# A 64-row contraction piece padded with zeros to 128 rows in the routed experts' return product

## The chip, the core and the metric

The kernel runs on one core of one Trainium2 chip. The metric is the device time of one execution in microseconds (us); lower is better. The kernel is one program for the whole model, and the change touches two of its six stages.

## What is computed

The input is 16 sequences of 256 tokens with 128 features. Six layers follow one another: a routed feed-forward, a retention layer, the routed feed-forward again, a relative-attention layer with its own experts, a plain attention and the relative layer again. The change lies in the routed feed-forward. Cut to what matters, it is:

```python
capacity = int(T / E * CAPACITY_FACTOR)            # 256 tokens / 8 experts * 1.25 = 40
scales = softmax(h @ rW3 + rb3)                    # router, three dense layers
topk_scales, topk_experts = top_k(scales, 2)
pos = ...                                          # place of each token in its expert's queue
keep = pos < capacity
dispatched = zeros((E, B, capacity, C)).at[e_flat, b_idx, pos_c].set(where(keep, x_rep, 0))
hh = relu(einsum('ebnc,ech->ebnh', dispatched, eW1) + eb1)
eout = einsum('ebnh,ehc->ebnc', hh, eW2) + eb2
out = sum(topk_scales[..., None] * where(keep, eout[e_flat, b_idx, pos_c], 0), axis=2)
x = x + 0.5 * out
```

The last two lines bring the experts' outputs back to the tokens. For one sequence there are 8 experts x 40 places = 320 slots, and each token's result is a weighted sum over those 320 slots (at most two weights are not zero).

## The kernel before

`routed_ffn` (line 107 on) is called twice, as stage f1 (from the start of the program) and as stage f3 (after the retention stage). It works on 8 groups of 2 sequences; a group is 4 tiles of 128 tokens (`GT = 4`). Its outer loop runs over steps s = 0 to 10, written out by hand for each engine. In step s the router works on group s, group s - 1 gets its slots, and the experts work on a pair of groups q two steps later. Each engine carries out its own list in the order written, and semaphores tie the lists together.

The return product is `back(q, half)` on TensorE (PE in the profile). It multiplies the slot weights of a group (`gts`, slots x tokens) with the experts' outputs (`eos`, slots x features). The contraction runs over 320 slots, and TensorE contracts at most 128 rows at once, so it is cut in three pieces:

```python
CHUNKS = [(first, min(P, S - first)) for first in range(0, S, P)]   # (0,128) (128,128) (256,64)
NW, WHOLE, LEFT = len(CHUNKS), S // P, S % P                        # 3, 2, 64
```

For each of the 4 token tiles `back` issues three matmuls of 128, 128 and 64 rows, which add up in one PSUM region. The operands are fp32, and the trace shows each such matmul as two, so that one `back` is 24 matmuls in the trace, all at line 358. The two `back` of a pair q stand in the even steps 4, 6, 8 and 10. In steps 4 and 6 the order on PE is: turning of the experts' outputs (`turn_slots`, line 345), a router product (`layer2`, lines 254 to 258), `back` of the first half, `count` (lines 290, 291), a router product (lines 214 to 216), `back` of the second half, `slots` (line 300), then `hidden` (line 312). In step 8 the router has ended and its products fall out; in step 10 only `turn_slots` and the two `back` are left.

What `back` gives is taken by VectorE (DVE) in `residual` (line 708), which adds half of it to `x`. In steps 4, 6 and 8 VectorE then does `place` (lines 657 and 662), which makes the table `f_d` that `slots` on TensorE needs; `count` needs `f_mask` (line 649). In step 10 a memset (line 763) stands between the two `residual`, and GpSimd (POOL) has one more (line 851).

The operands of `back` are written by copies from PSUM: lines 505, 506 (ScalarE, ACT) and 702, 703 (VectorE) for `eos`, lines 497, 498 and 696, 697 for the three buffers of `gts`. Lines 506, 703, 498 and 697 write only rows 0 to 63 of the third piece. One buffer of `gts` is `f_gts`; the other two lie in a tile that another stage owns, and appear as `all_qs`.

GpSimd's list starts with `ln_root(0)` (lines 800, 802: the reciprocal root for the layer norm), `rest_of_x(0)` (line 813) and four `rest_of_h1(0, m)` (line 819); then its loop over steps begins with `ln_root(1)`. VectorE's `ln_apply(1)` (line 597) waits for `ln_root(1)`, and TensorE's `turn_x(1)` (line 209) waits for `ln_apply(1)`.

Of the kernel before, what the change touches and what calls it, by code (L numbers as in the profile page):

```python
# [27 lines left out]
P = 128  # L28
B, T, C = 16, 256, 128
TT = T // P  # L30
# [3 lines left out]
KH = HID // P  # L34
# [72 lines left out]
def routed_ffn(nc, tag, x_sb, k, w):  # L107
# [3 lines left out]
    CHUNKS = [(first, min(P, S - first)) for first in range(0, S, P)]  # L111
    NW, WHOLE, LEFT = len(CHUNKS), S // P, S % P
    XW = NB * CAP
    W = GT * P
    HR, KR = 4, 3
    x_g = x_sb[:, :, :].rearrange("p (g t) c -> p g t c", t=GT)
    with ExitStack() as ctx:
        a = Pool_(nc, ctx, tag)
# [18 lines left out]
        eos, own = a.sb("eos", [P, NB, NW, C]), a.sb("gts", [P, GT, NW, P])  # L137
        stack = [k.qs[:, n, :, :].rearrange("p h t -> p (h t)").bitcast(F32) for n in range(2)]
        turned = [half[:, 0:GT * NW * P].rearrange("p (t v c) -> p t v c", t=GT, v=NW) for half in stack]
        gts = [turned[0], own, turned[1]]  # L140

        orders = {"ra": [], "rv": [], "ea": [], "ev": []}
        for s in range(G + 3):
            group, q, e = s - 1, (s - 2) // 2, 4 * (s % 2)
# [35 lines left out]
        def ring(name):  # L180
            taken = a.sem(f"{name}_taken")
            names = {item for item, _ in orders[name]}
            return Bench(a.ps(name, [P, 2, 512]), a.sem(f"{name}_filled"), {item: taken for item in names}, orders[name])

        ra, rv, ea, ev = ring("ra"), ring("rv"), ring("ea"), ring("ev")
        ra_taken, rv_taken, ea_taken, ev_taken = ra.emptied["x"], rv.emptied["h1"], ea.emptied["slots"], ev.emptied["slots"]
        (ln_stats, ln_aggr, ln_veps, ln_rstd, xn_ready, top_ready, lg_ready, ex_ready, den_step, sc_ready, best_step,
         mask_step, off_ready, d_ready, g_ready, xt_ready, h1_ready, zeroed, ks_zeroed) = [a.sem(n) for n in (
             "ln_stats ln_aggr ln_veps ln_rstd xn_ready top_ready lg_ready ex_ready den_step sc_ready best_step "
             "mask_step off_ready d_ready g_ready xt_ready h1_ready zeroed ks_zeroed").split()]  # L190
        block = ctx.enter_context(nc.Block())
        ROUTE = (ra, rv, ra, rv)
        EXPERT = (ea, ev)
# [1 line left out]
        @block.sync  # L195
        def _(sp):
            if w.load is not None:
                w.load_router(sp)
                w.load_rest(sp)
                w.load(sp)  # L200
                w.load_positions(sp)

        @block.tensor
        def _(pe):
# [144 lines left out]
            def back(q, half):  # L349
                g = 2 * q + half  # L350
                ev.free(pe, "back", (q, half))
                for b in range(2):
                    EXPERT[b].done(pe, "eos", (q, 2 * half + b))
                ea.done(pe, "weights", (g, 2))
                ev.done(pe, "weights", (g, 3))
                for t in range(GT):
                    for v, (first, rows) in enumerate(CHUNKS):
                        mm = nc.tensor.matmul(ev.bank("back", (q, half))[:, t * P:(t + 1) * P], gts[g % KR][0:rows, t, v, :],
                                              eos[0:rows, 2 * half + t // TT, v, :], start=(v == 0), stop=(v == NW - 1))
                mm.then_inc(ev.filled, 1)  # L360

            pe.wait_ge(k.loaded, k.loaded_count)
            for s in range(G + 3):
                group, q, e = s - 1, (s - 2) // 2, 4 * (s % 2)
# [35 lines left out]
                else:  # L400
# [4 lines left out]
                    if closed:  # L405
                        back(q - 1, 0)
# [4 lines left out]
                    if closed:  # L411
                        back(q - 1, 1)
# [383 lines left out]
        @block.gpsimd  # L796
        def _(pool):
            def ln_root(g):
                pool.wait_ge(ln_aggr, g + 1)
                nc.gpsimd.tensor_tensor(veps[:, :], mv[:, :, 1], k.eps[:, 0:GT], ALU.add).then_inc(ln_veps, 1)  # L800
                pool.wait_ge(ln_veps, g + 1)
                nc.gpsimd.tensor_tensor(rstd[:, :], veps[:, :], k.minus_half[:, 0:GT], ALU.pow).then_inc(ln_rstd, 1)

            def weigh(g):
                EXPERT[1].full(pool, "slots", (g, 1))
                nc.gpsimd.tensor_tensor(d[:, :, :], d[:, :, :], sc[:, :, :].rearrange("p t e -> p (t e)").unsqueeze(2)
                                        .to_broadcast([P, GT * E0, CAP]), ALU.mult).then_inc(g_ready, 1)

            def rest_of_x(g):
                ra.done(pool, "x", g)  # L810
                if g:
                    ROUTE[3].full(pool, "h1", (g - 1, 3))
                nc.gpsimd.tensor_tensor(xt_lo[:, :], xt[:, :], xt_hi[:, :], ALU.subtract).then_inc(xt_ready, 1)

            def rest_of_h1(g, m):
                ROUTE[m].done(pool, "h1", (g, m))
                if g:
                    ROUTE[3].full(pool, "h2", (g - 1, 3))
                nc.gpsimd.tensor_tensor(h1_lo[:, m, :], h1[:, m, :], h1_hi[:, m, :], ALU.subtract).then_inc(h1_ready, 1)

            pool.wait_ge(k.loaded, k.loaded_count)
            ln_root(0)
            rest_of_x(0)
            for m in range(KH):
                rest_of_h1(0, m)
            for s in range(G + 1):
                if s < G - 1:
                    ln_root(s + 1)
                if s and s % 2 == 0:
                    weigh(s - 1)  # L830
                if s < G - 1:
                    rest_of_x(s + 1)
                if s % 2:
                    weigh(s - 1)
                if s < G - 1:
                    for m in range(KH):
                        rest_of_h1(s + 1, m)
                if s == 1 and w.load is not None:
                    pool.wait_ge(h1_ready, 3 * KH)
                    for n, rows in enumerate((slice(32, 64), slice(64, ROWS))):  # L840
                        nc.gpsimd.memset(w.ws[rows, :, :, :].rearrange("p a h t -> p (a h t)"), 0.0).then_inc(w.ws_zeroed, 1)
                        pool.wait_ge(w.ws_zeroed, n + 1)
            pool.wait_ge(g_ready, G)
            if w.load is not None:
                for n, rows in enumerate((slice(32, 64), slice(64, ROWS))):
                    nc.gpsimd.memset(k.ks[rows, :, :, :].rearrange("p a h t -> p (a h t)"), 0.0).then_inc(ks_zeroed, 1)
                    pool.wait_ge(ks_zeroed, n + 1)
            for n, (last, tile, rows) in enumerate((((G // 2 - 2, 1), stack[1], slice(32, 64)), ((G // 2 - 2, 1), stack[1], slice(64, ROWS)),
                                                    ((G // 2 - 1, 0), stack[0], slice(64, ROWS)))):
                EXPERT[1].full(pool, "back", last)  # L850
                nc.gpsimd.memset(tile[rows, :], 0.0).then_inc(zeroed, 1)
                pool.wait_ge(zeroed, n + 1)
# [2403 lines left out]
def program(nc, io, stages=(1, 2, 3, 4, 5, 6)):  # L3256
    with ExitStack() as ctx:
        a = Pool_(nc, ctx, "all")
        x_sb = a.sb("x", [P, B * TT, C])
        k = constants(nc, a, io["cst"])  # L3260
        w = Weights()
        positions_weights(nc, a, io, w)
        with ExitStack() as layer:
            layer0_weights(nc, Pool_(nc, layer, "l0"), io, w)
            load_x(nc, k, io["x"], x_sb, w)
            if 1 in stages:
                routed_ffn(nc, "f1", x_sb, k, w)
                w.load = None
            if 2 in stages:
                retention(nc, "r2", x_sb, k, io)  # L3270
            if 3 in stages:
                routed_ffn(nc, "f3", x_sb, k, w)
        with ExitStack() as early:
            b = Pool_(nc, early, "a5b")
            x2t = b.sb("x2t", [P, B * TT, P])
            begun = Forerun(nc, b, "a5b", x_sb, k, io, x2t)
            relative_ffn(nc, "f4", x_sb, k, w, io, x2t=x2t, then=begun)
            relative_ffn(nc, "f6", x_sb, k, w, io, lambda lead, room: plain_attention(nc, "a5", x_sb, k, io, begun, lead, room), x2t=x2t,
                         out=io["out"])
# [75 lines left out]
```

## Time and profile before

| | |
|---|---|
| three timed runs | 3012.8, 3013.13, 3018.33 us; median 3013.13 us |
| the profiled execution: its own time, its span | 3010.51 us, 3008.5 us |
| mean granted TensorE clock | 0.974 |
| busy share of the span: PE, weight loads, DVE, ACT, POOL | 94%, 75%, 65%, 62%, 68% |

The span is the time from the first to the last instruction of one profiled execution; it is the time against which rows are set. Stage f1 takes the first 308 us of it, stage f3 the stretch from 523 to 820 us. A matmul's row shows its start and a modelled end: matmuls overlap, one of 128 columns is shown with some 275 ns, and the next starts long before that has passed. So the pace is read from start to start, not from the duration. "PEld" rows are the weight loads that belong to the matmuls; "idle before" in brackets names what an engine waited for.

### The profile page before, as it was taken

How to read it: one execution, taken by the hardware profiler on the slowest of the kernel's cores; microseconds unless marked ns; L12 is line 12 of the kernel's file. 1: busy time of each engine (PE TensorE's matmuls, PEld its weight loads, DVE VectorE, ACT ScalarE, POOL GpSimd, SP SyncE). 2: the span in 40 equal slices, each digit the busy share in tenths (PEclk: the TensorE clock that was granted, in tenths of full speed). 3: DMA queues.
4: the chain of work that ended last, by engine and by line, in shares of the span. 5: the costliest groups of instructions: out<-in, count | busy, mean ns of one | idle time of the engine just before them, and what ended most of it. 6: DMA issues, size and time to landing. Idle time of an engine off the chain costs nothing. (4 is left out here: it accounts for less than half of the span.)

```text
span 3008.5 us, 61670 instructions
## 1 busy us (share of the span) xinstructions
PE 2831.6 (94%) x20928; PEld 2262.6 (75%) x20928; DVE 1950.5 (65%) x4370; ACT 1851.2 (62%) x5109; POOL 2033.7 (68%) x2542
## 2 busy tenths in 40 slices
PE   7999797899879999998999989998999999999999
PEld 5888565688768888886788856665888888778887
DVE  5554587445458888886555566774888888755554
ACT  2333343333269999996444446777999999754444
POOL 4323664323168888876999974555888888689998
PEclk9999899999989999999999989999999999999999
DMA  3000464000032222222554555552222222255554
GB/s 109 6 1 1 115 142 98 1 1 1 10 64 44 43 44 54 54 58 104 182 193 185 188 166 118 113 104 47 43 50 58 43 44 43 57 205 194 195 194 165
DMA packets 152505, 266.05 MB, mean 88 GB/s; under 512 B 14098, under 2 KB 124946, under 8 KB 129138
## 3 DMA queue, kind: packets, MB, share of 16 engines
q1 hardware_dynamic: 152194, 262.11, 31.1%
q8 instruction: 170, 2.79, 0.4%
q14 instruction: 141, 1.16, 0.1%
HBM read 204.06 MB, written 53.67 MB: 86 GB/s over the span
## 5 line engine op out<-in xcount | busy, mean ns | idle before, releaser
L3144 POOL TENSOR_TENSOR f4m_ht_lo<-f4m_ht,f4m_ht_hi 128x512 fp32r<-128x512 f32 x256 | 331.0, 1311 | 38.2 <-ACT f4m_ht_hi L3069 29.0
L3144 POOL TENSOR_TENSOR f6m_ht_lo<-f6m_ht,f6m_ht_hi 128x512 fp32r<-128x512 f32 x256 | 331.2, 1307 | 32.3 <-ACT f6m_ht_hi L3069 20.2
L3114 DVE SCALAR_TENSOR_TENSOR f6m_ht<-f6m_hr,f6m_gate 128x512 f32<-128x512 f32 x256 | 176.3, 690 | 168.0 <-PE f6m_hr L2991 104.5
L3114 DVE SCALAR_TENSOR_TENSOR f4m_ht<-f4m_hr,f4m_gate 128x512 f32<-128x512 f32 x256 | 175.6, 690 | 162.3 <-PE f4m_hr L2991 101.9
L3069 ACT ACTIVATE f4m_ht_hi<-f4m_ht 128x512 fp32r<-128x512 f32 x256 | 161.6, 632 | 193.1 <-DVE f4m_ht L3114 192.8
L3069 ACT ACTIVATE f6m_ht_hi<-f6m_ht 128x512 fp32r<-128x512 f32 x256 | 161.7, 632 | 191.2 <-DVE f6m_ht L3114 191.0
L2665 ACT ACTIVATE f4a_pr<-f4a_sr,f4a_nm 128x256 f32<-128x256 f32 x512 | 243.7, 497 | 23.3 <-DVE f4a_nm L2733 22.8
L2665 ACT ACTIVATE f6a_pr<-f6a_sr,f6a_nm 128x256 f32<-128x256 f32 x512 | 243.6, 496 | 21.2 <-DVE f6a_nm L2733 20.5
L2819 POOL TENSOR_TENSOR f4a_rr<-f4a_tmp 128x256 f32<-128x256 f32 x256 | 186.7, 729 | 92.5 <-DVE f4a_tmp L2741 91.3
L2819 POOL TENSOR_TENSOR f6a_rr<-f6a_tmp 128x256 f32<-128x256 f32 x256 | 186.8, 730 | 82.8 <-DVE f6a_tmp L2741 81.6
L2741 DVE TENSOR_TENSOR f4a_tmp<-f4a_ur,f4a_turn 128x512 f32<-128x512 f32 x256 | 175.1, 685 | 61.2 <-PE f4a_ur L2530 57.4
L1997 DVE TENSOR_REDUCE a_nm<-a_sr 128x2 f32<-128x512 f32 x256 | 166.9, 684 | 69.3 <-PE a_sr L1730 68.2
L2733 DVE TENSOR_REDUCE f6a_nm<-f6a_sr 128x2 f32<-128x512 f32 x256 | 175.8, 687 | 50.5 <-PE f6a_sr L2547 49.6
L2733 DVE TENSOR_REDUCE f4a_nm<-f4a_sr 128x2 f32<-128x512 f32 x256 | 175.8, 687 | 50.1 <-PE f4a_sr L2547 49.3
L2741 DVE TENSOR_TENSOR f6a_tmp<-f6a_ur,f6l_turn 128x512 f32<-128x512 f32 x256 | 175.1, 684 | 49.2 <-PE f6a_ur L2530 46.6
L2825 POOL TENSOR_TENSOR f6a_rr_lo<-f6a_rr,f6a_rr_hi 128x256 fp32r<-128x256 f32 x256 | 190.4, 744 | 1.3 <-ACT f6a_rr_hi L2706 1.3
L2825 POOL TENSOR_TENSOR f4a_rr_lo<-f4a_rr,f4a_rr_hi 128x256 fp32r<-128x256 f32 x256 | 190.4, 744 | 0.9 <-ACT f4a_rr_hi L2706 0.9
L2545 PE MATMUL f4a_sr<-f4a_pe_hi,f4a_rr_hi 128*128 128x256 f32 x512 | 187.6, 366 | 0.0
L2545 PE MATMUL f6a_sr<-f6l_pe_hi,f6a_rr_hi 128*128 128x256 f32 x512 | 187.5, 366 | 0.0
L2557 PE MATMUL f6a_tr<-all_table,f6a_pr 128*128 128x128 f32 x1024 | 153.6, 272 | 0.3 <-ACT f6a_pr L2665 0.3
L2557 PE MATMUL f4a_tr<-all_table,f4a_pr 128*128 128x128 f32 x1024 | 153.5, 272 | 0.3 <-ACT f4a_pr L2665 0.3
L2542 PE MATMUL f4a_sr<-all_ks,all_qs 96*128 96x256 bf16 x512 | 143.4, 280 | 5.8 <-POOL f4a_rr_lo L2825 3.6
(585 smaller groups left out, 9368.5 us busy)
## 6 DMA issues: line engine op xcount, KB each, us to landing
f4m_gate<-f4o_gates SPq DMA_DIRECT2D x64, 1024.0 KB, 4.7
f6m_gate<-f6o_gates SPq DMA_DIRECT2D x64, 1024.0 KB, 4.7
r_scratch<-r_parts SPq DMA_DIRECT2D x32, 192.0 KB, 2.2
all_qs<-r_scratch SPq DMA_DIRECT2D x16, 384.0 KB, 4.9
all_ks<-r_scratch SPq DMA_DIRECT2D x16, 384.0 KB, 6.8
f4al_scratch<-f4a_parts SPq DMA_DIRECT2D x32, 192.0 KB, 2.2
all_qs<-f4al_scratch SPq DMA_DIRECT2D x16, 384.0 KB, 4.9
all_ks<-f4al_scratch SPq DMA_DIRECT2D x16, 384.0 KB, 6.7
```

Source lines behind the costliest of these rows:

```text
L1997: nc.vector.tensor_reduce(nm[:, r // 2, t, at_:at_ + 2], sr[:, g % SB, :].rearrange("p (x s) -> p x s", x=2), AX.X, ALU.max, negate=True). ...
L2542: nc.tensor.matmul(out, qs[0:ROWS, lead.buffer(b[0]), h, t * P:(t + 1) * P], ks[0:ROWS, lead.buffer(b[0]), h, :], start=True, stop=False)
L2545: nc.tensor.matmul(out, rr_hi[at], pe_hi[:, :], start=False, stop=False)
L2557: mm = nc.tensor.transpose(ring.bank(b, n // 2)[:, o:o + P], pr[:, n % 4, x, st * P:(st + 1) * P], k.ident)
L2665: last = nc.scalar.activation(pr[:, n % 4, x, :], sr.bank(b, n)[:, x * T:(x + 1) * T], ACT.Exp, bias=nm[:, n % SB, x:x + 1], accum_out=zs[ ...
L2733: nc.vector.tensor_reduce(nm[:, n % SB, :], sr.bank(b, n).rearrange("p (x s) -> p x s", x=2), AX.X, ALU.max, negate=True).then_inc(nm_read ...
L2741: nc.vector.tensor_tensor(tmp[:, hs % 2, :, :], ur.bank(b, hs).rearrange("p (u t) -> p u t", u=2), turn[:, :, :], ALU.mult).then_inc(ur.em ...
L2819: nc.gpsimd.tensor_tensor(rr[:, hs % RAW, :], tmp[:, hs % 2, 0, :], tmp[:, hs % 2, 1, :], ALU.add)\
L2825: nc.gpsimd.tensor_tensor(rr_lo[:, hs % RRS, :], rr[:, hs % RAW, :], rr_hi[:, hs % RRS, :], ALU.subtract)\
L3069: nc.scalar.activation(ht_hi[:, n % RB, :], ht[:, n % RB, :], ACT.Copy).then_inc(hi_ready, 1)
L3114: nc.vector.scalar_tensor_tensor(ht[:, n % RB, :], hr[:, n % HB, :], 0.0, gate[:, q % GB, n % LOADED, :], ALU.max, ALU.mult).then_inc(ht_r ...
L3144: nc.gpsimd.tensor_tensor(ht_lo[:, n % RB, :], ht[:, n % RB, :], ht_hi[:, n % RB, :], ALU.subtract)\
```

## The change

The third piece is contracted over 128 rows as the others are. Rows 64 to 127 of its operands are filled with zeros, so that the product is the same. GpSimd writes these zeros once per stage, into `eos` and the three buffers of `gts`: four memsets of 64 partitions x 4 x 128 fp32. They stand behind the four `rest_of_h1(0, m)` and ahead of `ln_root(1)`, and each waits for the one before it. TensorE waits for all four (`padded` at 4) before the first `back` of the stage. The copies that write rows 0 to 63 stay as they are, and nothing writes rows 64 to 127 later in the stage.

```diff
@@ back, on TensorE
+                if q == 0 and half == 0:
+                    pe.wait_ge(padded, 1 + KR)
                 for t in range(GT):
-                    for v, (first, rows) in enumerate(CHUNKS):
-                        mm = nc.tensor.matmul(ev.bank("back", (q, half))[:, t * P:(t + 1) * P], gts[g % KR][0:rows, t, v, :],
-                                              eos[0:rows, 2 * half + t // TT, v, :], start=(v == 0), stop=(v == NW - 1))
+                    for v in range(NW):
+                        mm = nc.tensor.matmul(ev.bank("back", (q, half))[:, t * P:(t + 1) * P], gts[g % KR][:, t, v, :],
+                                              eos[:, 2 * half + t // TT, v, :], start=(v == 0), stop=(v == NW - 1))
@@ GpSimd's list
             for m in range(KH):
                 rest_of_h1(0, m)
+            pool.wait_ge(h1_ready, KH)
+            for n, tile in enumerate([eos] + gts):
+                nc.gpsimd.memset(tile[LEFT:P, :, WHOLE, :], 0.0).then_inc(padded, 1)
+                pool.wait_ge(padded, n + 1)
             for s in range(G + 1):
                 if s < G - 1:
                     ln_root(s + 1)
```

`padded` is also added to the list of the stage's semaphores. GpSimd's list at the start of stage f1, before (`f_h_lo` is written by `rest_of_h1`, `f_veps` and `f_rstd` by `ln_root(1)`):

```order
L819 TENSOR_TENSOR f_h_lo<-f_h,f_h_hi 128x512 [waits load_table_in]
L819 TENSOR_TENSOR f_h_lo<-f_h,f_h_hi 128x512 [waits f1_rv_taken]
L800 TENSOR_TENSOR f_veps<-f_mv,all_half 128x4 [waits f1_ln_aggr]
L802 TENSOR_TENSOR f_rstd<-f_veps,all_half 128x4 [waits f1_ln_veps]
L813 TENSOR_TENSOR f_xt_lo<-f_xt,f_xt_hi 128x512 [waits f1_rv_filled,load_table_in]
```

and in the changed kernel (lines are some lines further down there):

```order
L821 TENSOR_TENSOR f_h_lo<-f_h,f_h_hi 128x512 [waits load_table_in]
L821 TENSOR_TENSOR f_h_lo<-f_h,f_h_hi 128x512 [waits f1_rv_taken]
L830 MEMSET f_eos 64x4x128 [waits f1_h1_ready]
L830 MEMSET all_qs 64x4x128 [waits f1_padded]
L830 MEMSET f_gts 64x4x128 [waits f1_padded]
L830 MEMSET all_qs 64x4x128 [waits f1_padded]
L802 TENSOR_TENSOR f_veps<-f_mv,all_half 128x4 [waits f1_ln_aggr,f1_padded]
L804 TENSOR_TENSOR f_rstd<-f_veps,all_half 128x4 [waits f1_ln_veps]
L815 TENSOR_TENSOR f_xt_lo<-f_xt,f_xt_hi 128x512 [waits f1_rv_filled,load_table_in]
```

Four instructions come in, and what followed stands four places later. On TensorE nothing moves. The piece of its list around the first `back` of the stage, with the old rows and the new ones:

```order
 L255 MATMUL f_ra<-f_h_hi,l_rw_lo 128x512
 L258 MATMUL f_ra<-f_h_lo,l_rw_hi 128x512 [waits f1_h1_ready] x4
-L358 MATMUL f_ev<-f_eos,all_qs 128x128 [waits f1_ea_taken,f1_ev_taken]
-L358 MATMUL f_ev<-f_eos,all_qs 128x128 x11
+L360 MATMUL f_ev<-f_eos,all_qs 128x128 [waits f1_ea_taken,f1_ev_taken,f1_padded]
+L360 MATMUL f_ev<-f_eos,all_qs 128x128 x11
 L291 MATMUL f_rv<-f_mask,all_bf 128x8 [waits f1_mask_step,f1_rv_taken]
 L290 MATMUL f_rv<-f_mask,all_bf 128x8
```

The twelve matmuls of a `back` keep their place and number; the first of the stage has one more semaphore to wait for, and every third one now has 128 rows.

## Rows read from the trace of the kernel before

**Rows 1.** Busy time by stretch, f1 and f3: length, busy us (count) per engine, PE clock.
```profile
118.00:308.00 190.00, 185.31 (x1126) 154.30 (x1125) 91.11 (x305) 55.61 (x148) 61.85 (x37) 1.00 0.00 1
628.00:823.00 195.00, 187.40 (x1137) 155.96 (x1135) 91.83 (x310) 56.05 (x148) 48.81 (x39) 1.00 0.01 2
```

**Rows 2.** Waits of PE from 118 to 310 us: us in total, times, longest.
```profile
PE f_ea L312 <- issue: 1.9, 3, 0.6
PE f_ea L345 <- issue: 0.8, 1, 0.8
```

**Rows 3.** Line 358 in f1 by shape: count, busy us, mean ns, idle before.
```profile
L358 PE MATMUL f_ev<-f_eos,all_qs 128*128 128x128 f32 x80 | 13.9, 296 | 0.2 <-DVE f_eos L703 0.2
L358 PE MATMUL f_ev<-f_eos,all_qs 64*128 64x128 f32 x40 | 9.7, 323 | 0.0
```

**Rows 4.** Timeline, weight loads of the first `back`, step 4: start, length in us, count.
```profile
133.90 0.29 PEld L358 LDWEIGHTS f_ev<-f_eos,all_qs 64*128 64x128 f32 x2
134.32 0.52 PEld L358 LDWEIGHTS f_ev<-f_eos,all_qs 128*128 128x128 f32 x4
134.96 0.29 PEld L358 LDWEIGHTS f_ev<-f_eos,all_qs 64*128 64x128 f32 x2
```

**Rows 5.** Timeline, TensorE around the two `back` of step 4.
```profile
133.37 4.19 PE L358 MATMUL f_ev<-f_eos,all_qs 128*128 128x128 f32 x24
...
137.49 0.18 PE L291 MATMUL f_rv<-f_mask,all_bf 128*128 128x8 bf16 x1
...
140.53 4.19 PE L358 MATMUL f_ev<-f_eos,f_gts 128*128 128x128 f32 x24
```

**Rows 6.** Timeline, step 4: `residual`, `place`, then `slots` on TensorE.
```profile
137.60 0.69 DVE L708 SCALAR_TENSOR_TENSOR all_x<-f_ev,all_x 128x512 f32<-128x512 f32 x1 [2.99 <-PE f_ev L358]
...
138.42 1.49 DVE L662 TENSOR_TENSOR f_d<-all_table,f_pos 128x1280 f32<-128x1280 f32 x1
...
144.65 1.34 PE L300 MATMUL f_ea<-f_d,f_xn 128*128 128x320 f32 x4
```

**Rows 7.** Timeline, step 8: `back`, mask, `residual`, `place`, `slots`.
```profile
265.25 4.27 PE L358 MATMUL f_ev<-f_eos,f_gts 128*128 128x128 f32 x24 [0.21 <-ACT f_eos L506]
...
267.56 0.18 DVE L649 TENSOR_SCALAR f_mask<-f_left 128x32 bf16<-128x32 f32 x1
...
269.56 0.69 DVE L708 SCALAR_TENSOR_TENSOR all_x<-f_ev,all_x 128x512 f32<-128x512 f32 x1 [1.60 <-PE f_ev L358]
...
270.38 1.49 DVE L662 TENSOR_TENSOR f_d<-all_table,f_pos 128x1280 f32<-128x1280 f32 x1
...
273.83 1.34 PE L300 MATMUL f_ea<-f_d,f_xn 128*128 128x320 f32 x4
```

**Rows 8.** Timeline, step 10, end of f1, and the next stage's first memset.
```profile
298.35 4.27 PE L358 MATMUL f_ev<-f_eos,all_qs 128*128 128x128 f32 x24 [0.21 <-DVE f_eos L703]
...
302.65 0.69 DVE L708 SCALAR_TENSOR_TENSOR all_x<-f_ev,all_x 128x512 f32<-128x512 f32 x1 [3.86 <-PE f_ev L358]
302.73 1.80 POOL L851 MEMSET all_qs<- 32x2048 f32 x1 [6.41 <-PE f_ev L358]
303.82 1.76 DVE L763 MEMSET all_qs<- 32x2048 f32 x1 [0.48 <-issue]
306.88 0.69 DVE L708 SCALAR_TENSOR_TENSOR all_x<-f_ev,all_x 128x512 f32<-128x512 f32 x1 [1.29 <-PE f_ev L358]
308.43 3.52 POOL L1329 MEMSET r_vm<- 128x4096 f32 x1 [3.90 <-POOLq L75]
```

**Rows 9.** Timeline, start of f1: `ln_root(1)`, `ln_apply(1)`, `turn_x(1)`.
```profile
20.09 0.20 POOL L800 TENSOR_TENSOR f_veps<-f_mv,all_half 128x4 f32<-128x4 f32 x1
...
20.38 1.02 POOL L802 TENSOR_TENSOR f_rstd<-f_veps,all_half 128x4 f32<-128x4 f32 x1
...
24.20 1.11 DVE L597 TENSOR_SCALAR f_xn<-all_x,f_mv,f_rstd 128x128 f32<-128x128 f32 x4
...
28.93 0.60 PE L209 MATMUL f_ra<-all_table,f_xn 128*128 128x128 f32 x4
```

More of the change, by code:

```diff
@@ L187, in routed_ffn @@
         (ln_stats, ln_aggr, ln_veps, ln_rstd, xn_ready, top_ready, lg_ready, ex_ready, den_step, sc_ready, best_step,
-         mask_step, off_ready, d_ready, g_ready, xt_ready, h1_ready, zeroed, ks_zeroed) = [a.sem(n) for n in (
+         mask_step, off_ready, d_ready, g_ready, padded, xt_ready, h1_ready, zeroed, ks_zeroed) = [a.sem(n) for n in (
              "ln_stats ln_aggr ln_veps ln_rstd xn_ready top_ready lg_ready ex_ready den_step sc_ready best_step "
-             "mask_step off_ready d_ready g_ready xt_ready h1_ready zeroed ks_zeroed").split()]
+             "mask_step off_ready d_ready g_ready padded xt_ready h1_ready zeroed ks_zeroed").split()]
         block = ctx.enter_context(nc.Block())
```

## The prediction

> **What bounds the kernel now.** I read the stretches first, then the waits of TensorE inside them, then the matmuls of line 358 by shape, then the single rows around them. In both routed stages the stretch with all the `back` (steps 4 to 10) keeps TensorE busy for 185 of 190 us and 187 of 195 us, at a granted clock of 1.00, while VectorE, ScalarE and GpSimd are busy for under half of it [rows 1]. TensorE's waits there come to 2.7 us in two places, of 0.6 and 0.8 us each [rows 2], and two of 0.21 us before a `back` [rows 7, 8]. So TensorE's own list sets the time of these stretches, and a microsecond taken out of that list is a microsecond of the kernel, as long as nothing that does not itself wait for the shortened part is late.
>
> A busy share says nothing of whether the time is well spent. The shapes of line 358 show a mean of 296 ns with 128 rows and 323 ns with 64 [rows 3], which looks like a small matter. But a duration here is a modelled end; the pace is in the starts. The four weight loads of two 128-row matmuls start at 134.32 and take 0.52 us together [rows 4]; one load is 0.19 us (0.29 us for a pair that starts 0.11 apart reads the same), so (0.52 - 0.19) / 3 = 0.11 us from start to start. That is the pace with no change of shape. After the four comes a pair with 64 rows at 134.96, that is 0.64 us after 134.32 where four times 0.11 would give 0.44. And a pair with 64 rows takes from 133.90 to 134.32, 0.42 us, where two times 0.11 would give 0.22 [rows 4]. Each change of the row count, in either direction, thus costs 0.2 us, and a token tile has two of them: 134.96 - 133.90 = 1.06 us for six matmuls instead of 0.67.
>
> **The change part by part.** *The `back` itself.* One `back` lasts from its first start to the start of what follows: 137.49 - 133.37 = 4.12 us [rows 5]. All 24 matmuls now have 128 rows: 24 x 0.112 = 2.69 us (0.112 and not 0.11, the upper side of what 0.33 / 3 can be by its rounding). It saves 1.43 us. The second one of step 4, 140.53 to 144.65, is 4.12 us too [rows 5, 6]. There are two in each of steps 4, 6, 8 and 10, eight per stage, 16 in all. The pace of a long run of 24 such matmuls isn't shown before, only runs of four; the bounds are 0.107, the lower side of the rounding, and 4.12 / 24 = 0.172, the mean pace of today's mix, which would save 1.55 us and nothing. I take 0.112, since the row nearest to the new list is the one of four equal shapes.
>
> Does the wall follow? *Steps 4 and 6.* `count` waits for the mask, which is there long before. `slots` waits for `place`: in step 4 VectorE waits 2.99 us for the first `back`, then has `f_d` ready at 138.42 + 1.49 = 139.91, and `slots` starts at 144.65 [rows 6]. With both `back` shortened, `slots` could start at 141.79; even an `f_d` that did not move would be there by then. Both savings are kept: 2.86 us per step.
>
> *Step 8.* Here no router product lies between. The first `back` starts at 265.25; `count` then comes at about 265.25 + 2.77 = 268.02 (0.08 more, since this `back` starts after a wait), and the mask is written until 267.56 + 0.18 = 267.74, 0.28 us before. The residual starts at about 268.2 instead of 269.56, and `f_d` ends 2.31 us after that start (270.38 + 1.49 - 269.56), at 270.5. The second `back` ends its starts at about 268.19 + 2.77 = 270.96, so `slots` finds `f_d` 0.4 us old [rows 7]. Both savings are kept, with little room.
>
> *Step 10.* The two `back` run one after the other, so VectorE's first residual moves from 302.65 to about 301.2 and the memset behind it from 303.82 to 302.4, ending at 304.15. The second `back` would let the second residual start 2.86 us early, at 304.0; the memset now ends last. So it starts at 304.15 instead of 306.88: 2.7 us are kept. GpSimd's memset (302.73, 1.80 us) moves along and stays hidden [rows 8].
>
> The stage after starts from a barrier behind these and moves as a whole. Per stage 3 x 2.86 + 2.7 = 11.3 us, for two 22.6 us.
>
> *The memsets.* GpSimd's rows show 1.80 us for 2048 fp32 per partition and 3.52 us for 4096 [rows 8], 0.88 ns per element, with 32 or 128 partitions alike. 512 elements make 0.45 us, four make 1.8, with about 0.1 us between two dependent instructions (20.09 + 0.20 to 20.38 [rows 9]) 2.2 us. They push `ln_root(1)`, which ends at 20.38 + 1.02 = 21.40, to 23.6. `ln_apply(1)` starts at 24.20, because VectorE is at other work: hidden. If the memsets cost more, `turn_x(1)` comes only at 28.93 and `ln_apply` takes 1.11, so `ln_root(1)` may end as late as 27.7 [rows 9]: 6.3 us of cover. The bounds: nothing, and four times the nearest longer row, 7.2 us, which would be 0.9 us late, 1.8 us for two stages. I take nothing. No other engine waits for GpSimd in between, and TensorE's new wait is for something done 100 us before. Stage f3 has the same order at its start.
>
> **Rule and row.** The 64-row matmuls stand off from the 128-row ones by 0.2 us each way [rows 4]. The Trainium skill, "TensorE: Matmul & The Clock Gate", section "LDWEIGHTS (loading the stationary operand)", says the opposite of a gain: a weight load's time goes by its columns, and one of 32 rows takes as long as one of 128; the table in "Why this matters for your kernels" says the same of a single matmul. By that rule padding changes nothing, and the sum would be 0. The rows bear the rule out for the load by itself (0.29 us for a pair) but not for the pace across a change of shape, which is what this kernel pays for.
>
> **The sum.** The profiled execution took 3010.5 us by its own time; less 22.6 that is 2987.9. The median of the timed runs is 3013.1, 2.6 above it, so I predict 2990.5 us.
>
> **The rivals.** *No difference.* A matmul costs by its columns, and the gaps of 0.2 us belong to something else that comes every six matmuls (the new token tile's operands and output). Against it: the gap stands before the 64-row pair as well, inside a tile, where operands and output region go on as before. If only the shown durations differed, 64 x 0.027 us x 2 stages = 3.5 us [rows 3] for the fp32 pairs: 3009.6, which no measurement tells from no change (the bound is 0.2%, 6 us). Chance 0.05.
>
> *A new wait takes part of it.* VectorE's chain mask, residual, `place` becomes the last in step 8 and its memset in step 10, where the room is 0.3 to 0.4 us and none. If the second saving in both steps were lost, 4 x 1.43 less the 0.3 already counted = 5.4 us: 2995.9. For it: the small margins of rows 7 and 8; against it: each link of the chain itself waits for the first `back`, which is earlier too. Chance 0.10.
>
> *Slower.* The memsets on GpSimd hold up `ln_root(1)`, with it `ln_apply(1)` and `turn_x(1)`. Place: the start of f1 and of f3. If one cost the 3.52 us of the longest memset on this engine [rows 8], four would end at 34.3, `ln_root(1)` at 35.5, 7.8 us after the last harmless moment: 15.6 us in both stages. It decides from 1.6 us per memset on, and makes the kernel slower where the gain on TensorE is smaller than the delay, at worst 3013.1 + 15.6 = 3028.7. Against it: an eighth of the elements. Chance 0.03.
>
> The forecast itself has a chance of 0.82.
>
> **How the numbers follow.** A pace of 0.107 us would save 16 x 0.12 = 1.9 us more (2988.6), the memsets at their upper bound 1.8 us less (2992.3), and runs of the kernel before lie up to 5 us apart. The new wait reaches to 2996. I give 2985 to 2998. Faster by over 0.2% are the forecast and the new wait: 0.92; within 0.2% 0.05; slower 0.03.
>
> **What would show it.** In the changed kernel's profile all rows of the return product have 128 rows, and one `back` of 24 reads about 2.8 us instead of 4.19; the first residual of step 4 waits about 1.6 us instead of 2.99; `slots` of step 4 comes 2.9 us sooner after the step's start; the stretch of steps 4 to 10 is 11 us shorter in each of the stages; four memsets of 64 partitions take about 0.5 us each, and `ln_apply(1)` stands where it stood. I am wrong if the rows keep gaps of 0.2 us between token tiles, if `slots` in step 8 waits for `f_d`, or if `turn_x(1)` starts later than before.

## The result

The changed kernel takes 2987.39 us (median of 4 runs, 2985.78 to 2989.39), the kernel before 3013.23 us (4 runs, 3012.8 to 3018.33). The ratio is 0.9911, with a 95% interval of 0.9894 to 0.9928: 25.8 us faster, where 2990.5 us were predicted and 2985 to 2998 was the range. The profiled execution took 2985.78 us with a span of 2983.8 us, 24.7 us less than the span before, at the same mean granted clock of 0.974.

### The profile page after: what moved, and what is told of

Its sections match the earlier page's. It is cut to its first block and busy times, and to the rows that moved or that the text cites. A ratio compares the mean times of both kernels' runs of the same rounds, so it can differ in the third digit from the quotient of the medians.

```text
span 2983.8 us, 61682 instructions
## 1 busy us (share of the span) xinstructions
PE 2806.0 (94%) x20928; PEld 2255.4 (76%) x20928; DVE 1951.9 (65%) x4370; ACT 1852.1 (62%) x5109; POOL 2039.4 (68%) x2550
```

## The profile after

The stretch that answers to [rows 1] for f1, steps 4 to 10, taken 11 us shorter since the stage ends that much earlier (columns as there):

```profile
118.00:297.00 179.00, 173.28 (x1125) 149.79 (x1123) 91.43 (x307) 55.47 (x148) 62.27 (x38) 1.00 0.00 1
```

TensorE is about as full as before (173.3 of 179 us, before 185.3 of 190): 12 us less busy time for nearly the same number of matmuls in the window (1125, before 1126). The length of a window is chosen; what is measured is the time from the first `back` of f1 to its last residual, 306.88 - 133.37 = 173.51 us before and 295.10 - 133.22 = 161.88 us now. The return product by shape and one stretch of its weight loads, answering to [rows 3] and [rows 4]:

```profile
L360 PE MATMUL f_ev<-f_eos,all_qs 128*128 128x128 f32 x120 | 14.4, 276 | 0.2 <-DVE f_eos L705 0.2
L360 PE MATMUL f_ev<-f_eos,f_gts 128*128 128x128 f32 x72 | 8.6, 276 | 0.2 <-ACT f_eos L508 0.2
```
```profile
133.44 0.41 PEld L360 LDWEIGHTS f_ev<-f_eos,all_qs 128*128 128x128 f32 x3
```

All 192 matmuls of the stage have 128 rows and a mean of 276 ns, and three weight loads at a boundary between the second and the third piece take 0.41 us: (0.41 - 0.19) / 2 = 0.11 us from start to start. Before, the load of the third piece stood 0.2 us behind that pace. The timeline around the two `back` of step 4 answers to [rows 5] and [rows 6]:

```profile
133.22 2.84 PE L360 MATMUL f_ev<-f_eos,all_qs 128*128 128x128 f32 x24
...
135.89 0.17 PE L291 MATMUL f_rv<-f_mask,all_bf 128*128 128x8 bf16 x1
...
136.09 0.69 DVE L710 SCALAR_TENSOR_TENSOR all_x<-f_ev,all_x 128x512 f32<-128x512 f32 x1 [1.63 <-PE f_ev L360]
...
136.91 1.49 DVE L664 TENSOR_TENSOR f_d<-all_table,f_pos 128x1280 f32<-128x1280 f32 x1
...
138.92 2.84 PE L360 MATMUL f_ev<-f_eos,f_gts 128*128 128x128 f32 x24
...
141.59 1.24 PE L300 MATMUL f_ea<-f_d,f_xn 128*128 128x320 f32 x4
```

One `back` lasts 135.89 - 133.22 = 2.67 us up to what follows, instead of 4.12. VectorE's residual waits 1.63 us for it instead of 2.99. The second one lasts 2.67 us too (138.92 to 141.59). And `slots` itself reads 1.24 us where it read 1.34: before, it was the first matmul after a 64-row one and paid for the change as well.

Step 8, answering to [rows 7]:

```profile
259.11 2.92 PE L360 MATMUL f_ev<-f_eos,f_gts 128*128 128x128 f32 x24 [0.21 <-ACT f_eos L508]
...
261.42 0.18 DVE L651 TENSOR_SCALAR f_mask<-f_left 128x32 bf16<-128x32 f32 x1
...
261.86 0.17 PE L291 MATMUL f_rv<-f_mask,all_bf 128*128 128x8 bf16 x1
...
262.06 0.69 DVE L710 SCALAR_TENSOR_TENSOR all_x<-f_ev,all_x 128x512 f32<-128x512 f32 x1 [0.25 <-PE f_ev L360]
262.88 1.49 DVE L664 TENSOR_TENSOR f_d<-all_table,f_pos 128x1280 f32<-128x1280 f32 x1
264.78 1.24 PE L300 MATMUL f_ea<-f_d,f_xn 128*128 128x320 f32 x4
```

The mask is written until 261.60 and `count` starts at 261.86; `f_d` ends at 264.37 and `slots` starts at 264.78. VectorE's work is ready 0.26 and 0.41 us ahead, so the two tight places held. Step 10 answers to [rows 8]:

```profile
289.20 2.92 PE L360 MATMUL f_ev<-f_eos,all_qs 128*128 128x128 f32 x24 [0.21 <-DVE f_eos L705]
...
291.95 2.84 PE L360 MATMUL f_ev<-f_eos,f_gts 128*128 128x128 f32 x24
...
292.15 0.69 DVE L710 SCALAR_TENSOR_TENSOR all_x<-f_ev,all_x 128x512 f32<-128x512 f32 x1 [2.51 <-PE f_ev L360]
292.23 1.80 POOL L857 MEMSET all_qs<- 32x2048 f32 x1 [5.06 <-PE f_ev L360]
293.32 1.76 DVE L765 MEMSET all_qs<- 32x2048 f32 x1 [0.48 <-issue]
295.10 0.69 DVE L710 SCALAR_TENSOR_TENSOR all_x<-f_ev,all_x 128x512 f32<-128x512 f32 x1
296.64 3.52 POOL L1335 MEMSET r_vm<- 128x4096 f32 x1 [2.61 <-POOLq L75]
```

The residual behind the memset carries no wait any more: it starts as the memset ends (293.32 + 1.76 = 295.08), and the last `back` has ended at 291.95 + 2.84 = 294.79. From the first `back` to that residual it takes 5.90 us instead of 8.53. The start of f1 answers to [rows 9]:

```profile
20.09 0.52 POOL L830 MEMSET f_eos<- 64x512 f32 x1
...
21.83 0.52 POOL L830 MEMSET all_qs<- 64x512 f32 x1
22.43 0.20 POOL L802 TENSOR_TENSOR f_veps<-f_mv,all_half 128x4 f32<-128x4 f32 x1
22.71 1.02 POOL L804 TENSOR_TENSOR f_rstd<-f_veps,all_half 128x4 f32<-128x4 f32 x1
...
24.10 1.10 DVE L599 TENSOR_SCALAR f_xn<-all_x,f_mv,f_rstd 128x128 f32<-128x128 f32 x4
...
28.83 0.60 PE L209 MATMUL f_ra<-all_table,f_xn 128*128 128x128 f32 x4
```

The four memsets take 0.52 us each and 0.58 from start to start, `ln_root(1)` ends at 23.73 instead of 21.40, and `ln_apply(1)` and `turn_x(1)` stand where they stood.

The sum of both stages can be read at the first instruction of VectorE behind f3, before and after:

```profile
821.14 0.49 DVE L2205 BATCH_NORM_STATS2 f4a_stats<-all_x 128x6 f32<-128x128 f32 x2 [1.50 <-PEq L75]
```
```profile
798.52 0.49 DVE L2211 BATCH_NORM_STATS2 f4a_stats<-all_x 128x6 f32<-128x128 f32 x2 [1.50 <-PEq L75]
```

821.14 - 798.52 = 22.6 us. The remaining 2.1 us of the 24.7 come up behind f3, where the two kernels do the same. The difference first falls to 21.5 us, jumps to 24.6 us at one instruction of the stage f4m and stays near that to the end. It is the same instruction of both lists; in the execution before it waited 4.45 us for a transfer, in the one after 1.54 us for GpSimd:

```profile
1775.14 1.29 DVE L3114 SCALAR_TENSOR_TENSOR f4m_ht<-f4m_hr,f4m_gate 128x512 f32<-128x512 f32 x2 [4.45 <-DMA f4m_gate<-f4o_gates]
```
```profile
1750.56 0.69 DVE L3120 SCALAR_TENSOR_TENSOR f4m_ht<-f4m_hr,f4m_gate 128x512 f32<-128x512 f32 x1 [1.54 <-POOL f4m_ht_lo L3150]
```

Nothing in the change touches that transfer. The kernel before, run 15 times beside e1 to e4 below, gave 3002.5 to 3014.9 us with a median of 3010.9, and 3008.9 to 3014.5 us in 7 runs beside e5 to e7; differences of this size lie between executions of one kernel.

## Experiments

Ratios are against the kernel before, run on the same chip in the same rounds (median 3010.9 us beside both sets). Since whole times of one kernel lie up to 12 us apart, the traces give a sharper measure, the time from the first `back` of a stage to its last residual, in f1 and in f3:

| | f1, us | f3, us |
|---|---|---|
| before | 173.51 | 173.52 |
| changed | 161.88 | 162.02 |
| e1, zeros without the wider product | 173.51 | 173.51 |
| e2, 96 rows | 161.91 | 161.95 |
| e3, 64-row pieces side by side | 167.84 | 167.84 |
| e4, 64 rows everywhere | 163.57 | 163.57 |
| e5, e6, more memsets | 161.90, 161.92 | 161.91, 162.05 |
| e7, 32 rows | 173.45 | 173.46 |

**Zeros without the wider product (e1).** The changed kernel with the old row counts:

```diff
-                        mm = matmul(..., gts[g % KR][:, t, v, :], eos[:, ..., v, :], ...)
+                        rows = CHUNKS[v][1]
+                        mm = matmul(..., gts[g % KR][0:rows, t, v, :], eos[0:rows, ..., v, :], ...)
```

Expected: 

> The four memsets per stage and TensorE's wait stay, the return product goes back to 128, 128 and 64 rows. My theory (the whole gain is the missing change between 64 and 128 rows on TensorE, and the memsets are hidden): the time of the kernel before, ratio 1.000, 3013 us within 0.1%; 24 matmuls of a return product in 4.19 us. Rival A (the zeroed rows or the later ln_root shift the start of the stage): 3015 to 3018 us. Rival B (part of the gain is from somewhere else than the row count, for example the order at the stage's start): below 3009 us.

Measured: 3012.41 us (10 runs), ratio 1.0004 (0.9994 to 1.0015). The timeline of TensorE at the first `back`:

```profile
133.56 4.19 PE L361 MATMUL f_ev<-f_eos,all_qs 128*128 128x128 f32 x24
137.68 0.18 PE L291 MATMUL f_rv<-f_mask,all_bf 128*128 128x8 bf16 x1
```

4.12 us from the first start to `count`, as before. The interval of the ratio reaches from 3009 to 3015 us and so touches both rivals; the trace decides. The first `back` starts at 133.56 us (before 133.37), and both stages take from there on what they took before (table). The memsets and the wait cost at most that 0.2 us and bring nothing; the whole gain comes with the row count. Both rivals fall.

**96 rows instead of 128 (e2).**

```diff
-                        mm = matmul(..., gts[g % KR][:, t, v, :], eos[:, ..., v, :], ...)
+                        rows = 96 if v == WHOLE else P
+                        mm = matmul(..., gts[g % KR][0:rows, t, v, :], eos[0:rows, ..., v, :], ...)
```

Expected: 

> The third piece has 96 rows instead of 128 (rows 64 to 95 are zeros). Theory 1 (the array has a mode for up to 64 rows and one for more, and only a change of the mode costs): the time of the changed kernel, about 2987 us, 24 matmuls in 2.84 us. Rival (any change of the row count costs 0.2 us): the time of the kernel before, 3013 us, 24 matmuls in 4.19 us.

Measured: 2986.29 us (4 runs), ratio 0.992 (0.9905 to 0.9935), as the changed kernel. TensorE at the first `back` (timeline), and the third piece by shape:

```profile
133.60 2.84 PE L361 MATMUL f_ev<-f_eos,all_qs 128*128 128x128 f32 x24
136.28 0.17 PE L291 MATMUL f_rv<-f_mask,all_bf 128*128 128x8 bf16 x1
```
```profile
L361 PE MATMUL f_ev<-f_eos,all_qs 96*128 96x128 f32 x40 | 7.7, 274 | 0.0
```

2.68 us to `count`. The row count changes as often as in the kernel before, and nothing stalls. So it is not a change of the row count as such that costs: between 128 and 96 rows it is free, between 128 and 64 it is not. Where between 64 and 96 rows the border lies, no run shows, and of the reason I know only this.

**The 64-row pieces side by side (e3).** The kernel before, with the order of the pieces turned round in every second token tile:

```diff
-                    for v, (first, rows) in enumerate(CHUNKS):
-                        mm = matmul(..., start=(v == 0), stop=(v == NW - 1))
+                    order = (WHOLE, *range(WHOLE)) if t % 2 else range(NW)
+                    for n, v in enumerate(order):
+                        rows = CHUNKS[v][1]
+                        mm = matmul(..., start=(n == 0), stop=(n == NW - 1))
```

Expected: 

> The kernel before, without zeros, but in every second token tile the 64-row piece comes first instead of last, so that two of them stand side by side: 4 changes between 64 and 128 rows per return product instead of 8, with the same number of 64-row matmuls. Theory (each change costs about 0.19 us): a return product saves 1.44 - 4 x 0.19 = 0.67 us, 16 of them 10.7 us: 3002.5 us. Rival (each 64-row piece costs, wherever it stands): no saving, 3013 us.

Measured: 3001.89 us (6 runs), ratio 0.997 (0.9958 to 0.9982), 9.0 us below the 3010.9 beside it, where 10.7 were expected; that the time itself was met so closely is chance, since it was counted from 3013. In the traces the two stages save 5.7 us each, 11.3 in all. TensorE at the first `back`, and the weight loads of its first four 64-row matmuls and of the eight 128-row ones behind them:

```profile
134.49 3.61 PE L360 MATMUL f_ev<-f_eos,all_qs 128*128 128x128 f32 x24
137.94 0.17 PE L291 MATMUL f_rv<-f_mask,all_bf 128*128 128x8 bf16 x1
```
```profile
135.02 0.52 PEld L360 LDWEIGHTS f_ev<-f_eos,all_qs 64*128 64x128 f32 x4
135.66 0.97 PEld L360 LDWEIGHTS f_ev<-f_eos,all_qs 128*128 128x128 f32 x8
```

A `back` lasts 137.94 - 134.49 = 3.45 us, 0.67 less than 4.12, as expected. Inside the block of four with 64 rows the loads start (0.52 - 0.19) / 3 = 0.11 us apart, as with 128 rows; between 135.02 and 135.66 there is again 0.2 us too much (0.64 for four). With as many 64-row matmuls as before and half the changes, about half the cost is gone: 3.45 - 2.67 = 0.78 us are left for four changes, 0.195 us each. The rival, a price per 64-row piece, falls.

**64 rows everywhere (e4).**

```diff
-                        mm = matmul(..., gts[g % KR][0:rows, t, v, :], eos[0:rows, ..., v, :], ...)
+                        mm = matmul(..., gts[g % KR][0:LEFT, t, v, :], eos[0:LEFT, ..., v, :], ...)
```

Expected: 

> All three pieces of a return product contract 64 rows only, so rows 64 to 127 of the first two pieces are left out of the sum; no zeros, no memsets. Theory (64 rows are as quick as 128 once the mode is set; there are two changes per return product, at its ends): 24 matmuls at 0.11 us, plus about 0.3 us at the ends, 2.85 to 3.0 us up to what follows: 16 x 0.3 = 5 us above the changed kernel, 2991 to 2993 us. Rival (a matmul with 64 rows is itself slow, 0.2 us from start to start): 24 x 0.2 = 4.9 us per return product, 16 x 0.7 = 12 us above the kernel before: 3025 us.

Measured: 2992.77 us (4 runs), ratio 0.994 (0.9926 to 0.9955).

```profile
133.37 2.94 PE L358 MATMUL f_ev<-f_eos,all_qs 64*128 64x128 f32 x24
136.24 0.18 PE L291 MATMUL f_rv<-f_mask,all_bf 128*128 128x8 bf16 x1
```

2.87 us to `count`: 0.2 us more than with 128 rows, for the changes at the ends. Both stages together take 3.2 us more than in the changed kernel (table); 5 were expected, and that the time of 2992.77 us fits them is chance, as whole times lie further apart than that. A matmul with 64 rows is as quick as one with 128, once no change lies ahead of it. The rival of 3025 us falls.

**16 memsets per stage (e5) and 8 (e6).** The changed kernel:

```diff
-            for n, tile in enumerate([eos] + gts):
+            for n, tile in enumerate(([eos] + gts) * 4):        # e6: * 2
```

and TensorE waits for 16 (e6: 8). Expected of e5: 

> The changed kernel with its four memsets carried out four times over, 16 per stage one after the other at 0.58 us from start to start (as its trace shows for four). Theory (the memsets are hidden as long as ln_root(1) ends 6.3 us or less after its time before, at about 27.7 us of the span): 16 x 0.58 = 9.3 us from 20.09, ln_root(1) ends at 30.7, turn_x(1) starts at 31.9 instead of 28.8; 3.1 us late in each of the two stages: 2987 + 6 = 2993 us. Rival (GpSimd has room all the way, the delay is absorbed by later waits of TensorE in step 1): 2987 us.

Expected of e6: 

> The changed kernel with its four memsets carried out twice, 8 per stage: 4.6 us, ln_root(1) ends at 26.0 us. Theory (cover up to 27.7): as the changed kernel, 2987 us within 1 us, turn_x(1) at 28.8. Rival (the cover is only that up to ln_apply(1), which starts at 24.1 in the changed kernel, since VectorE's list is held up behind it): 2 us later per stage, 2991 us.

Measured: e5 2994.27 us (4 runs), ratio 0.9946 (0.9931 to 0.9961); e6 2986.92 us (4 runs), ratio 0.9914 (0.9897 to 0.9932), as the changed kernel. Timelines of e5 and of e6 at the start of f1:

```profile
28.79 0.52 POOL L830 MEMSET all_qs<- 64x512 f32 x1
...
29.67 1.02 POOL L804 TENSOR_TENSOR f_rstd<-f_veps,all_half 128x4 f32<-128x4 f32 x1
30.72 1.11 DVE L599 TENSOR_SCALAR f_xn<-all_x,f_mv,f_rstd 128x128 f32<-128x128 f32 x4 [6.53 <-POOL f_rstd L804]
...
31.98 0.63 PE L209 MATMUL f_ra<-all_table,f_xn 128*128 128x128 f32 x4 [2.98 <-DVE f_xn L599]
```
```profile
25.20 1.02 POOL L804 TENSOR_TENSOR f_rstd<-f_veps,all_half 128x4 f32<-128x4 f32 x1
26.25 1.11 DVE L599 TENSOR_SCALAR f_xn<-all_x,f_mv,f_rstd 128x128 f32<-128x128 f32 x4 [1.91 <-POOL f_rstd L804]
...
28.98 0.60 PE L209 MATMUL f_ra<-all_table,f_xn 128*128 128x128 f32 x4
```

In e6 `ln_apply(1)` is 2.15 us later than in the changed kernel, and `turn_x(1)` starts at 28.98 (28.93 in the kernel before): VectorE's place was not the limit, the cover reaches on to TensorE. In e5 `turn_x(1)` starts at 31.98, 3.15 us late, with 31.9 forecast. The whole is 7.4 us slower than e6, where 6 were expected. The forecast of 3.1 us per stage was too small all the same, for the delay grows behind `turn_x(1)`. TensorE from 30 to 40 us, in e5 and then in the changed kernel (length, busy us, granted clock), and the first `back` of e5:

```profile
30.00:40.00 10.00, 7.38 (x24) 0.66 0.01 2
```
```profile
30.00:40.00 10.00, 8.29 (x40) 1.00 0.01 2
```
```profile
138.60 2.84 PE L360 MATMUL f_ev<-f_eos,all_qs 128*128 128x128 f32 x24
```

After TensorE had stood still for 2.98 us ahead of `turn_x(1)`, the granted clock of these 10 us was 0.66 instead of 1.00, and the router's matmuls behind it (lines 214 to 216) started 0.43 us apart instead of 0.23. By the first `back` the 3.15 us had become 138.60 - 133.22 = 5.4 us. In f3 it is the same: VectorE is 6.5 us behind the changed kernel ahead of `ln_apply(1)` and the first `back` 12.1 us, 5.6 more (granted clock 0.61 from 543 to 556 us, against 1.00 in the same place of the changed kernel, 533 to 546 us). The whole span of e5 is 8.7 us longer than the changed kernel's and not 12, since the stages behind f3 took 2182.0 us in this execution against 2185.3; they took 2184.9 to 2190.2 us in the other traces, and why they were shorter here no run shows.

**32 rows in the third piece (e7).**

```diff
                     for v, (first, rows) in enumerate(CHUNKS):
+                        rows = min(rows, 32) if v == WHOLE else rows
```

Expected: 

> The kernel before with 32 rows in the third piece instead of 64 (rows 32 to 63 of it are left out of the sum), to see what other partial row counts cost; one look. Theory (a change between the whole array and a part of it costs the same whatever the part): 24 matmuls in 4.19 us, the time of the kernel before, 3010 us. Rival (the cost grows with the distance in rows): over 4.5 us for the 24, 3015 us or more.

Measured: 3017.3 us in a single run.

```profile
134.45 4.18 PE L359 MATMUL f_ev<-f_eos,all_qs 128*128 128x128 f32 x24
138.56 0.18 PE L291 MATMUL f_rv<-f_mask,all_bf 128*128 128x8 bf16 x1
```

The 24 matmuls take 4.18 us, and 138.56 - 134.45 = 4.11 us up to `count`, as with 64 rows: a change to 32 rows costs what one to 64 costs. The single run lies 6 us above the median of the kernel before, though its two stages from the first `back` on do not (table). Against the trace of the kernel before the excess lies where no edit is: 1.1 us ahead of the first `back`, 3.1 us between the two stages, 2.8 us behind f3. There it took 341.6 us between the stages and 2190.2 us behind f3, just above the spread of the other traces without e5 (335.9 to 341.2 us and 2184.9 to 2188.4 us). With one run the cause of that stays open; the return product is not it.

## Why the prediction was right

- *The `back` itself.* Predicted 4.12 to 2.69 us, measured 4.12 to 2.67. The pace of a run of 24 was taken from runs of four, and it held. That changes between 64 and 128 rows are the cause was argued then; e1, e3 and e4 show it, since the time follows the number of changes and neither the zeros nor the number of 64-row matmuls. My words "each change of the row count" were too wide: 96 rows cost nothing (e2).
- *Steps 4 and 6.* Both savings kept, as predicted: 1.63 us of wait at the residual, where 1.6 was said. `slots` gains another 0.1 us, which the sum did not have, since I cut the cost of the last change at the start of the next matmul. It is three such places per stage.
- *Step 8.* Room of 0.28 and 0.4 us predicted, 0.26 and 0.41 measured. The rival of a new wait was near, and did not come.
- *Step 10.* Predicted 2.7 us with the memset as the last to end; measured 8.53 - 5.90 = 2.63, and the residual's row has no wait.
- *The memsets.* 2.2 us predicted, 2.3 measured, hidden; e6 and e5 place the end of the cover between 8 and 16 of them, and e5's delay of `turn_x(1)` agrees with a last harmless moment at 27.7 us (`ln_root(1)` ends at 30.69, and `turn_x(1)` is 3.15 us late). The slower rival needed 1.6 us per memset, and one takes 0.52. Its price was too low, though: it counted a late `turn_x(1)` at its length, and in e5 3.15 us of it cost 5.4.
- *The sum.* 22.6 us predicted for both stages and 22.6 measured behind f3. The exact agreement is luck: from the first `back` to the last residual f1 saves 11.6 us and f3 11.5, 23.1 where 22.6 were predicted (`slots` and the 0.02 us per `back` make the difference), and the stretches ahead of each stage's first `back` took 0.5 us more together in the execution after. The time of 2987.39 us lies 3.1 us below the 2990.5 predicted: 2.1 us came up behind f3, and 1.0 us is that the profiled execution lies 1.6 us below its median here and lay 2.6 below it before. Both are of the size by which executions of one kernel differ; against the median of 3010.9 us in the later rounds, e6 and e2, which issue as many matmuls and stall as little, are 24.0 and 24.6 us faster.
- *A reading that was off.* The 2.7 us of TensorE's waits in [rows 2] are four waits, three at line 312 with 1.9 us in all and one at line 345 with 0.8, not two. Nothing in the sum rests on it.
- *The rule against it.* The Trainium skill, "TensorE: Matmul & The Clock Gate", section "LDWEIGHTS (loading the stationary operand)", holds for a matmul among its like (e4: 64 rows at the pace of 128) and not at a change. The page "TensorEngine Tiling (Array Packing)" of the Trainium skill, section "Key Properties", has the other half: a switch of the tiling mode drains the engine. Its section "Available Configurations" lists modes of 128, 64 and 32 rows. That no mode has 96 rows fits e2, which loses nothing, and e7 fits as well, where 32 rows lose what 64 do. The traces show the time lost and not what the engine does in it.

## What to carry to other kernels

Read the pace of matmuls from start to start and by neighbours, not from the mean duration: here the mean showed 27 ns per matmul and the starts 0.2 us per change. When a contraction is cut into pieces and a last one of 64 or 32 rows stands between full ones, fill it up with zeros written once (here 96 rows did as well as 128), or let short pieces stand side by side. Check that what waits behind the shortened product is ready; here 0.26 us of room decided that all of it counted.

## What the runs showed of the hardware that I had not expected

- A change between 128 and 64 rows costs 0.2 us of TensorE in fp32 at a granted clock of 1.00, in either direction (e3: 0.78 us for four); 128 and 96 rows mix at the full pace of 0.11 us (e2), and 32 rows cost what 64 do (e7).
- GpSimd's memset goes by the elements per partition and not by the number of partitions, as far as these rows show: 0.52 us for 64 partitions x 512 fp32, 1.80 us for 32 x 2048, 3.52 us for 128 x 4096.
- A wait of TensorE early in a stage can cost more than its length: behind 2.98 us of standstill the granted clock of 10 us was 0.66 instead of 1.00, and 3.15 us of delay became 5.4 (e5).
